# A three-stage graph network on one core: two-source forms for three vector instructions, and another order of the work within a pair

## The reference, cut to what matters

```python
h = relu(layernorm(x))
g = gcn_conv(h, W1, b1); g = gelu(layer_norm(g, gamma1, beta1))
g = gcn_conv(g, W2, b2); g = layer_norm(g, gamma2, beta2)
x = x + gelu(g + h)                       # the "residual" of stage 2 is h
h = relu(layernorm(x))
x = x + gcn_conv(h, W3, b3)               # stage 3
# gcn_conv: out[d] = dinv[d] * (dinv[d]*(xW)[d] + sum over edges of dinv[s]*(xW)[s]) + b
```

## Time and profile before

| what | us |
|---|---|
| median of 3 runs | 3602.36 (3601.42 to 3603.95) |
| the profiled execution | 3601.81 |
| its span, first to last instruction | 3599.8 |
| busy: PE / DVE / POOL / ACT | 3057.2 / 3139.7 / 2095.7 / 1650.5 |
| stage 1, steady part | from 449 to 1396 |
| stage 2, with its start | from 1404 to 2554 |
| stage 3, with its start | from 2559 to the end |

### The profile page before, as it was taken

How to read it: one execution, slowest core, us unless ns; L and a number is a source line. 1 busy time by engine, 2 the same in 40 slices (tenths; PEclk the granted TensorE clock), 3 DMA queues, 4 the chain that set the end, 5 groups by cost and what they waited for, 6 DMA issues and landing times. The chain is left out here.

```text
span 3599.8 us, 61879 instructions
## 1 busy us (share of the span) xinstructions
PE 3057.2 (85%) x16897; PEld 2498.2 (69%) x16897; DVE 3139.7 (87%) x6745; ACT 1650.5 (46%) x2375; POOL 2095.7 (58%) x1853
## 2 busy tenths in 40 slices
PE   8133299999999997999999999999488888888888
PEld 2022188888888886777777777778477777777777
DVE  9899789999999996888888888888688888888887
ACT  0366445555555553777777777777311111111111
POOL 0122256556556654677777777777466666666665
PEclk9999999999999998999999999999799999999999
DMA  3499967777777775888888888888477777777775
GB/s 118 163 408 418 365 215 221 220 225 222 218 223 223 220 219 171 289 295 299 297 296 295 296 298 295 297 295 288 162 241 246 241 246 242 241 246 238 246 240 190
DMA packets 277302, 914.70 MB, mean 254 GB/s; under 512 B 47617, under 2 KB 49511, under 8 KB 277246
## 3 DMA queue, kind: packets, MB, share of 16 engines
q1 hardware_dynamic: 191614, 683.15, 53.1%
q0 software_dynamic: 85632, 230.90, 22.9%
HBM read 653.47 MB, written 308.59 MB: 267 GB/s over the span
## 5 line engine op out<-in xcount | busy, mean ns | idle before, releaser
L840 POOL DMA_INDIRECT g<-H,idx x1062 | 1212.3, 1142 | 614.8 <-issue 428.9
L895 ACT ACTIVATE ahi<-agg 128x1024 fp32r<-128x1024 f32 x354 | 360.9, 1019 | 1039.1 <-PE agg L1171 1039.1
L1189 PE MATMUL out<-Whi,ahi 128*128 128x512 f32 x2832 | 768.9, 393 | 0.0
L1189 PE MATMUL out<-Wlo,ahi 128*128 128x512 f32 x2832 | 763.6, 391 | 0.0
L1189 PE MATMUL out<-Whi,alo 128*128 128x512 f32 x2832 | 761.2, 391 | 0.5 <-DVE alo L1006 0.5
L1162 PE MATMUL agg<-ident,self 128*128 128x128 f32 x2832 | 474.5, 279 | 220.9 <-DVE self L998 171.9
L1189 PEld LDWEIGHTS out<-Wlo,ahi 128*128 128x128 f32 x2832 | 531.6, 188 | 119.6
L1189 PEld LDWEIGHTS out<-Whi,alo 128*128 128x128 f32 x2832 | 531.6, 188 | 114.1 <-DVE alo L1006 1.0
L1189 PEld LDWEIGHTS out<-Whi,ahi 128*128 128x128 f32 x2832 | 510.4, 189 | 91.1
L1162 PEld LDWEIGHTS agg<-ident,self 128*128 128x128 f32 x2832 | 339.3, 142 | 315.8 <-DVE self L998 220.6
L1171 PE MATMUL agg<-sv,vhi 128*128 128x256 f32 x1416 | 384.0, 304 | 66.2 <-DVE sv L986 66.2
(11 more groups left out here) (175 smaller groups left out, 4137.5 us busy)
## 6 DMA issues: line engine op xcount, KB each, us to landing
self<-H SPq DMA_DIRECT2D x351, 512.0 KB, 5.1
H<-ho SPq DMA_DIRECT2D x250, 512.0 KB, 4.2
x<-in_x_dram SPq DMA_DIRECT2D x165, 512.0 KB, 6.2
X<-x SPq DMA_DIRECT2D x117, 512.0 KB, 4.3
x<-X SPq DMA_DIRECT2D x117, 512.0 KB, 7.2
out_dram<-conv SPq DMA_DIRECT2D x117, 512.0 KB, 6.3
H<-x SPq DMA_DIRECT2D x48, 512.0 KB, 9.6
g<-H,idx POOLq DMA_INDIRECT x1062, 4.3
```

The costliest lines, as they stand in the source:

```text
L840: pool.indirect_dma_start(g[:, c, :], None, H[q][0:end, :], bass.IndirectOffsetOnAxis(ap=own[:, c:c + 1], axis=0), bounds_check=end - 1, o ...
L895: nc.scalar.activation(Ahi[p.slot(2)][:, :], Agg[p.slot(2)][:, :], ACT.Copy)\
L1189: m = nc.tensor.matmul(o, a[u][:, c:c + P], w[q][:, f, :], start=(n == 0), stop=(third and n == 3 * KD - 1))
```

## The change

Three DVE instructions get a second tensor as an operand, `ones` or a new constant tile `eps_c`: `sv`, `x2_mean` and `x2_var_eps`. `ones` grows from 128 to 256 columns, and the ring of `oh_place` shrinks from four to three. In the bodies: DVE now begins with `add_first` and `over_low` of p+2 (in this order, before: `over_low` first, and both behind `normal`); in stage 1 `low` moves behind `stats`; in stage 2 `x2_mean` follows `x2_sum` at once (before: behind `stats`). On ACT `relu_x` moves ahead of `gelu` and `relu_x2`. Three start-up orders change too.

```diff
-        ones = sb("ones", [P, P])
+        ones = sb("ones", [P, 2 * P])
+        eps_c = sb("eps_c", [P, 2])
-        oh_place = [sb(f"oh_place{u}", [P, WINDOW], BF16) for u in range(4)]
+        oh_place = [sb(f"oh_place{u}", [P, WINDOW], BF16) for u in range(3)]
...
                 def place(n):
-                    if n >= 4:
-                        dve.wait_ge(place_used, n - 3)
+                    if n >= 3:
+                        dve.wait_ge(place_used, n - 2)
...  SP, at known == 0
                             for k in range(2):
                                 load_self(0, p.after(k), k)
                                 load_root(0, p.after(k), k)
+                            for k in range(2):
                                 load_x(0, p.after(k), k)
...  ACT body
                         if known == 0:
                             over_high(p)
+                            high(p)
                             over_high(p.after(1))
-                            high(p)
...
+                        if second and has(known, 0):
+                            relu_x(known, p)
                         if not third and has(known, -1):
                             gelu(p.after(-1))
...
                         if second and has(known, -2):
                             relu_x2(of(known, -2), p.after(-2))
-                        if second and has(known, 0):
-                            relu_x(known, p)
...  DVE
-                        nc.vector.tensor_scalar(Sv[...], col[:, :], over_to[...], None, ALU.is_equal)
+                        nc.vector.scalar_tensor_tensor(Sv[...], col[:, :], over_to[...],
+                                                       ones[:, :], ALU.is_equal, ALU.mult)
-                        nc.vector.tensor_scalar(m[:, 28:30], m[:, 24:26], -1.0 / D, None, ALU.mult)
+                        nc.vector.scalar_tensor_tensor(m[:, 28:30], m[:, 24:26], -1.0 / D, ones[:, 0:2],
+                                                       ALU.mult, ALU.mult)
-                        return nc.vector.tensor_scalar(m[:, 18:20], m[:, 26:28], 1.0 / D, EPS, ALU.mult, ALU.add)
+                        return nc.vector.scalar_tensor_tensor(m[:, 18:20], m[:, 26:28], 1.0 / D, eps_c[:, :], ALU.mult, ALU.add)
...  DVE body
                             for k in range(2):
-                                over_low(p.after(k))
                                 if added:
                                     add_first(p.after(k))
-                            low(p)
+                                over_low(p.after(k))
+                                if k == 0:
+                                    low(p)
+                        if has(known, 2):
+                            if added:
+                                add_first(p.after(2))
+                            over_low(p.after(2))
                         if second and has(known, -2):
                             x2_coefs(p.after(-2))
                         if not third and has(known, -1):
                             normal(of(known, -1), p.after(-1))
                         if has(known, 4):
                             indices(p.after(4))
-                        if has(known, 2):
-                            over_low(p.after(2))
-                            if added:
-                                add_first(p.after(2))
-                        if has(known, 1):
+                        if not first and has(known, 1):
                             low(p.after(1))
                         if second and has(known, -1):
                             x2_sum(of(known, -1), p.after(-1))
+                            x2_mean(p.after(-1))
...
                             stats(p)
-                        if second and has(known, -1):
-                            x2_mean(p.after(-1))
+                        if first and has(known, 1):
+                            low(p.after(1))
```

More of the change, by code:

```diff
@@ L366, in _ @@
                 nc.vector.memset(neg_half[:, :], -0.5)
+                nc.vector.memset(eps_c[:, :], EPS)
                 nc.vector.memset(has_first[:, :], 0.0)
@@ L539, in place @@
                     p, c = n // 3, n % 3
-                    if n >= 4:
-                        dve.wait_ge(place_used, n - 3)
-                    nc.vector.tensor_scalar(oh_place[n % 4][:, :], placeb[:, :], edge_place[:, c, p:p + 1], None,
+                    if n >= 3:
+                        dve.wait_ge(place_used, n - 2)
+                    nc.vector.tensor_scalar(oh_place[n % 3][:, :], placeb[:, :], edge_place[:, c, p:p + 1], None,
                                             ALU.is_equal).then_inc(place_made, 1)
@@ L599, in _ @@
                 pe.wait_ge(said_made, 1)
-                nc.tensor.matmul(bank[5][:, 0:2], ones[0:NPAIR, :], said[0:NPAIR, :], start=True, stop=True)\
+                nc.tensor.matmul(bank[5][:, 0:2], ones[0:NPAIR, 0:P], said[0:NPAIR, :], start=True, stop=True)\
                     .then_inc(summed, 1)
@@ L613, in _ @@
                     for k in range(3):
-                        m = nc.tensor.matmul(bank[3 + k][:, 4 * p:4 * p + 4], oh_place[n % 4][:, k * P:(k + 1) * P],
+                        m = nc.tensor.matmul(bank[3 + k][:, 4 * p:4 * p + 4], oh_place[n % 3][:, k * P:(k + 1) * P],
                                              edge_vals[:, c, p, :], start=(n == 0), stop=(n == 3 * NPAIR - 1),
@@ L985, in over_low @@
                                                 Vhi[p.slot(2)][:, :].bitcast(F32), ALU.subtract).then_inc(vlo_done.sem, 1)
-                        nc.vector.tensor_scalar(Sv[p.slot(2)][:, :], col[:, :], over_to[:, bass.ds(p.n, 1)],
-                                                None, ALU.is_equal).then_inc(sv_made.sem, 1)
+                        nc.vector.scalar_tensor_tensor(Sv[p.slot(2)][:, :], col[:, :], over_to[:, bass.ds(p.n, 1)],
+                                                       ones[:, :], ALU.is_equal, ALU.mult).then_inc(sv_made.sem, 1)
                     def add_first(p):
@@ L1071, in x2_mean @@
                         dve.wait_ge(x2_done.sem, x2_done.upto(p))
-                        nc.vector.tensor_scalar(m[:, 28:30], m[:, 24:26], -1.0 / D, None, ALU.mult)\
-                            .then_inc(mean2_done.sem, 1)
+                        nc.vector.scalar_tensor_tensor(m[:, 28:30], m[:, 24:26], -1.0 / D, ones[:, 0:2],
+                                                       ALU.mult, ALU.mult).then_inc(mean2_done.sem, 1)
                     def x2_var_eps(p):
```

## The result

The changed kernel takes 3701.48 us (median of 4 runs, 3697.89 to 3704.11) against 3601.89 for the kernel before on the same chip: a ratio of 1.0276 (95% interval 1.0259 to 1.0294), 99.6 us slower. Its profiled execution took 3701.54 us with a span of 3699.5.

What follows compares the result with a forecast made beforehand. Stage 1 was taken as at PE's floor, stage 2 as DVE's cycle, stage 3 as a loop through DVE. Sum: 3601.8 - 12 - 118 + 177 + 3 = 3652 us; range 3380 to 3710.

Steps and rivals of the forecast that it cites:

- Sign and mechanism: Whole kernel: slower, at 0.52; in stage 2 early `relu_x` makes `r` early, so POOL's additions stall `x2_sum`.
- Slipping through: Rival, stage 2: POOL's additions lose to both halves of `x2_sum`, no stall, period 8.8, total 3397; chance 0.31.
- half a stall: Rival, stage 2: DVE gets in between POOL's two additions, losing 1.3 instead of 2.6; total 3500; chance 0.10.
- stage 3 gives nothing: Rival, stage 3: `vlo` is held each time and gathers are drawn out, period stays 8.6, total 3770; chance 0.04.
- Stage 2, +177: Stage 2: period from 9.48 to 11.0 as additions stall `x2_sum`; 114 pairs give +177 us, bounds +116 and +219.
- PE's wait for `sv` in stage 2: Stage 2: PE's wait of 0.57 + 0.16 us goes away with `over_low` at the head.
- The hold that "begins up to 0.4 us before its row": POOL's additions hold DVE instructions with SBUF inputs, starting up to 0.4 us before the additions' row.
- The wait for squares: Stage 2: with `x2_mean` directly behind `x2_sum`, DVE's 1.28 us wait for ACT's squares shrinks to about 0.15.
- Stage 3, -118: Stage 3: `add_first` ahead of `over_low` takes the period from 8.64 to 7.6; -118 us, bounds -150 and -38.
- The form: Two-source `sv`: 0.43 against 0.379 us, +0.05 on DVE a pair, standing still beside POOL's additions as before.
- Stage 1, -12: Stage 1: DVE loses drains and PE's 0.09 wait goes; 115 pairs at 0.10 give -12 us, bounds 0 and -20.
- The ring of three, +3: Preparation: DVE waits for PE to finish the third tile before; 354 tiles, +3 us taken, bounds 0 and +35.

Runs made afterwards that it cites:

- a1: The changed kernel with only `relu_x` put back behind `relu_x2` on ACT; 3532.76 us, ratio 0.9806 to the kernel before.
- a4: The kernel before with only `relu_x` moved ahead of `gelu` on ACT in stage 2; 3900.28 us, ratio 1.0829.
- a2: The changed kernel with POOL's two stage-2 additions cut from 512 columns to 2; 3393.77 us, ratio 0.9421.
- b2: The changed kernel with waits timing POOL's additions in stages 2 and 3, and the index copy first in stage 3; 3427.81 us, ratio 0.9517.
- c1: The changed kernel in one-source forms, stage 3 as in b2, stage-2 additions timed and split between gathers, index copy first in stages 2 and 3; 3368.74 us.
- b1: The kernel before with `add_first` and `over_low` of p+2 at the head of DVE's body in stage 3 alone; 3459.84 us, ratio 0.9604.
- a3: The changed kernel with `sv`, `x2_mean` and `x2_var_eps` back in one-source form; 3655.45 us, ratio 1.0148 to the kernel before.
- c2: The kernel before with only the two-source `sv`, the wider `ones` and the ring of three; 3635.45 us, ratio 1.0095.

## Why the prediction was right, point by point

**Sign and mechanism: right, and shown.** The additions start with no wait for `r` and catch `x2_sum`. Undoing only that (a1) gives 169 us back, doing only that (a4) loses 298, shortening only the additions (a2) brings PE's floor, and with the additions moved (b2; c1, which also splits the gathers and has the old forms) the changed order beats the kernel before by 174 and 232. Slipping through (3397) and half a stall (3500) fell by the mean of 1973 ns over the halves: 2 x (1973 - 689) = 2.57 us a pair, the full length of both additions. That stage 3 gives nothing fell by 7.74. The size was right only in part: 50 us of loss were forecast and 99.6 measured, 8.5 under the top of the range, and nearly all that is missing lies in stage 2.

**Stage 2, +177 in the prediction, +214 measured: the mis-sized term.** (The +177 itself should read +173: 11.0 - 9.48 is 1.52.) The pair shown takes 11.41 (1805.99 to 1817.40), 0.41 more than the 11.0 forecast. I had added the additions' 2.6 to `x2_sum`'s own start, 5.25 after var_eps, so that its held half would end at 5.25 + 0.69 + 2.6 = 8.54. It ends at 8.81, and its own start (5.48, behind `gelu`'s end at 1811.24) isn't what decides that. In another pair, whose var_eps is at 1611.85, it starts at 5.29:

```profile
1617.14 3.50 DVE L1067 SCALAR_TENSOR_TENSOR x<-x,y 128x512 f32<-128x512 f32 x1
1617.56 2.52 POOL L854 TENSOR_TENSOR r<-r,vec 128x512 f32<-128x512 f32 x2
...
1623.22 0.16 DVE L1033 TENSOR_TENSOR small<-small,eps 128x2 f32<-128x2 f32 x1
```

It stands longer by as much and ends at 8.79, and the pair takes 11.37. (33 pairs with such a start have a mean period of 11.36, the other 81 of 11.42.) What decides is when the additions end. They start 5.71 after var_eps, because the first gather takes 1.55 instead of 1.07; in a4, where it takes 1.07, they start at 5.40 in the median and the held half ends at 8.49. The prediction had a start of 5.2 to 5.7, and drawn-out gathers in its upper bound, but its sum hung the stall on `x2_sum`'s start instead of on the additions' end: that is the step that was too small, by 0.27 us a pair. The other 0.15 is L1026's drain behind `stats`, which I hadn't counted, as the mean now goes ahead. Together they are the 0.41, 47 us.

**PE's wait for `sv` in stage 2** was forecast to go and is 2.56 us in the pair shown. That costs nothing by itself: PE's work fits into 8.78 us (a2) of the 11.42, and where the hold is gone (a2) so is the wait.

**The hold that "begins up to 0.4 us before its row": too general.** It holds where a gather ends just before the additions, as it does 0.02 us before those of the earlier trace rows. Where POOL had been idle, an instruction begun before the additions isn't held (`sv` at 1414.42). The forecast took its times from the earlier trace rows, where the gather was there, and so lost nothing by it.

**The wait for squares: right.** 1.28 went to nothing (I had 0.15), as `x2_mean` stands ahead of `stats`.

**Stage 3, -118 against -101: right in kind, the caught instruction not named.** I had the stall shared by `vlo`, `sv` and `self`; it falls on the index copy behind `sv`. In one-source form the same order runs at 7.46 (b1) and 7.41 (a3), so the form took 39 us of this stage's gain.

**The form: too cheap.** `sv` costs 0.10 more, not 0.05, and c2's 34 us are twice what 0.05 gives over 342 pairs, 17. That it is held beside the additions in either form was right (c2 3.17, before 3.05).

**Stage 1, -12 against -16: right.** The period is 7.82 with PE showing 200.00 busy in 200 us, so its floor was 0.07 lower than I worked out from the gaps. Why, no run here tells.

**The ring of three, +3:** the first index copy of stage 1 stands at 440.36 against 440.18, so it cost nothing that can be read.

## What to carry to other kernels

Before an instruction is moved forward on one engine, look up what its output releases on GpSimd and which DVE instruction is then running: here a `relu_x` begun 1.11 instead of 5.59 us after var_eps cost 169 us, though ACT had room for it. In this kernel GpSimd's additions belong beside DVE instructions that read PSUM, and a wait that puts them there is worth more than the idle time it makes. Look, too, at what GpSimd does right before them: right behind a gather the full-length additions held a DVE instruction already begun, after idle time they didn't. But leave what DVE waits for (`power`) ahead of them. And a change that loses as a whole may hold a good part: run its parts by themselves before it is thrown away.

## What the runs showed of the hardware

- The size of a DVE instruction is no protection: three int32 columns took 3.14 us beside the additions. The copy would have ended at 3009.08 and the additions' row starts at 3009.49; what ran on POOL meanwhile was the gather, until 3009.46.
- Gathers are drawn out when they begin under a DVE instruction that works on SBUF data: in the changed kernel the median gather begun under `vlo` alone took 1.43 us and the one begun under `self` in stage 3 1.75; in the kernel before the one begun under `self` in stage 1 took 1.79. Gathers begun under `alo` took 1.01 and those begun beside an idle DVE 1.00. The form of `sv` isn't the reason: in a3, one-source, the first gather of stage 2 takes the same 1.55. In the pair of c1 shown it begins within 0.01 us of `vlo` and takes 1.07.
- TensorE's granted clock was 0.95 in stage 2 of the changed kernel and 0.92 in a4, where PE waited over 2 us in each pair (2.56 before the first `sv` matmul of the pair shown), and 0.99 to 1.00 in a2, b2 and c1, where it didn't. Both are means of long stretches at 2.4 GHz and short ones at 1.2. I take it to have cost nothing, since DVE set the period and PE stood waiting; no run separates it.
